# A gated delta-rule block with 2:4-sparse feed-forward: the first step in an order of its own, and part of the feed-forward preparation in the first drain body

## The reference, cut to what matters

```python
mod = silu(c) @ wmod                      # 6 parts of 256: sa, ca, ga, sb, cb, gb, per batch
ga, gb = guard(ga), guard(gb)             # magnitude at least 0.25, sign kept
h = layernorm(x) * (1 + ca) + sa          # x: 8 batches x 256 tokens x 256
# attention, 16 key heads (128), 2 value heads (128) each
qkv, z = h @ W_qkv.T, h @ W_z.T
beta = sigmoid(h @ W_b.T); decay = exp(-softplus(h @ W_a.T + dt_bias) * exp(A_log))
qkv = causal 4-tap convolution of qkv; q, k = l2norm per head
for t in range(256):                      # delta rule, state 128 x 128 for each value head
    dv = beta[t] * (v[t] - k[t] @ S); S = S * decay[t] + outer(k[t], dv); o[t] = q[t] @ S
x = x + ga * ((rmsnorm(o) * norm_w * silu(z)) @ W_out.T)
h = layernorm(x) * (1 + cb) + sb
h = silu(h @ w_gate) * (h @ w_up)         # 1024 wide
h = of every 4 neighbours keep the 2 of largest magnitude
x = x + gb * (h @ w_down)
```

## Time and profile before

| what | value |
|---|---|
| median of 3 runs | 2014.25 us (2011.45 to 2016.29) |
| the profiled execution | 2010.74 us, its span 2009.0 us |
| busy share PE, DVE, ACT, POOL | 97%, 90%, 86%, 69% |
| instructions | 63635 |
| mean granted clock of PE | 0.988 |
| share of PE in the chain that ended last | 91% |

### The profile page before, as it was taken

The page is one execution under the profiler, slowest core; times in us unless marked ns, Lnnn a source line. Parts: engine busy times, 40 slices in busy tenths (PEclk is TensorE's granted clock), DMA queues, the critical chain, the costliest instruction groups (busy, mean ns, idle before and its releaser), DMA issues.

```text
span 2009.0 us, 63635 instructions
## 1 busy us (share of the span) xinstructions
PE 1947.9 (97%) x24518; PEld 1656.9 (82%) x24518; DVE 1800.0 (90%) x2901; ACT 1737.5 (86%) x3588; POOL 1382.2 (69%) x962
## 2 busy tenths in 40 slices
PE   6699999999999999999999999999999999997999
PEld 5478888888888888888888888888888888886787
DVE  6889999999999999999999999999999999985997
ACT  4699999999999999999999999999999999986332
POOL 6367777777777777777777777777777777764452
PEclk9799999999999999999999999999999999998899
DMA  3000000000000000000000000000000000003000
GB/s 117 13 23 3 3 24 3 24 2 24 3 24 3 24 2 4 22 3 23 3 24 3 24 3 24 3 24 2 3 24 3 24 3 2 24 3 115 6 27 22
DMA packets 17596, 35.75 MB, mean 18 GB/s; under 512 B 5772, under 2 KB 14092, under 8 KB 14996
## 3 DMA queue, kind: packets, MB, share of 16 engines
q1 hardware_dynamic: 17300, 31.68, 4.7%
HBM read 29.04 MB, written 2.64 MB: 16 GB/s over the span
## 4 chain that ended last, share of the span: by engine, by line
PE 91%; DVE 3%; POOL 2%; issue 2%; ACT 1%; DMA 0%; POOLq 0%; SPq 0%; DVEq 0%; ACTq 0%
PE bank L647 81%; PE bank L650 10%; DVE tt L1677 0%; ACT yl L1282 0%; DVE b_le L1667 0%; POOL a_lo L520 0%; DMA o<-in_x 0%; POOL go L541 0%; POOL invT L557 0%; POOL y_acc L564 0%; POOL osq L513 0%; DVE ae L1831 0%; DVE oss L1899 0%; POOL f_small L572 0%; POOL e_b L505 0%
## 5 line engine op out<-in xcount | busy, mean ns | idle before, releaser
L1796 DVE SCALAR_TENSOR_TENSOR cc<-bank,wc,cc 128x510 f32<-128x510 f32 (+2 forms) x768 | 558.7, 740 | 13.4 <-ACT cc L1307 3.7
L647 PE MATMUL bank<-h,w 128*128 128x512 f16 (+1 forms) x1920 | 422.4, 361 | 5.6 <-DVE cc L1796 5.5
L647 PEld LDWEIGHTS bank<-h,w 128*128 128x128 f16 x1920 | 173.9, 98 | 140.9 <-DVE cc L1796 6.6
L486 POOL TENSOR_TENSOR rn<-n2m,mhalf 128x4 f32<-128x4 f32 x64 | 64.8, 1012 | 280.8 <-DVE n2m L1812 280.8
L1392 ACT ACTIVATE inv<-bank 128x512 f16<-128x512 f32 x384 | 244.7, 637 | 11.5 <-PE bank L647 11.5
L1397 ACT ACTIVATE invT<-bank 128x512 f16<-128x512 f32 x384 | 246.5, 642 | 1.3 <-PE bank L647 1.3
L1860 DVE TENSOR_TENSOR yl<-bank,mask 128x512 f16<-128x512 f32 x320 | 218.9, 684 | 6.5 <-PE bank L647 6.4
L647 PE MATMUL bank<-inv,a 128*128 128x64 f16 (+1 forms) x3584 | 217.4, 197 | 4.1 <-ACT inv L1392 3.9
L1307 ACT ACTIVATE cc<-bank,wc 128x512 f32<-128x512 f32 x256 | 177.8, 695 | 33.3 <-PE bank L647 33.2
L647 PEld LDWEIGHTS bank<-inv,a 128*128 128x128 f16 x3584 | 179.7, 98 | 16.5 <-ACT inv L1392 5.2
L647 PE MATMUL bank<-w,goT 128*128 128x256 f16 x1536 | 190.8, 275 | 1.4 <-DVE goT L1912 1.4
(11 more groups left out here) (230 smaller groups left out, 5504.1 us busy)
## 6 DMA issues: line engine op xcount, KB each, us to landing
w_raw<-in_wh SPq DMA_DIRECT2D x15, 1032.0 KB, 5.0
v<-in_x SPq DMA_DIRECT2D x4, 512.0 KB, 4.0
out<-sol SPq DMA_DIRECT2D x16, 128.0 KB, 1.7
moving<-rank_store SPq DMA_DIRECT2D x64, 8.0 KB
standing<-rank_store SPq DMA_DIRECT2D x64, 8.0 KB
w_raw<-in_wgate SPq DMA_DIRECT2D x1, 1024.0 KB, 5.0
cc<-in_wup SPq DMA_DIRECT2D x1, 1024.0 KB, 4.8
pt<-gate_store SPq DMA_DIRECT2D x2, 512.0 KB, 5.1
```

Source lines behind the costliest of these rows:

```text
L486: gp.tensor_tensor(rn[:], n2m[:, blk(s), 0], mhalf[:, 0:TL], ALU.pow).then_inc(sig("rn"), 1)
L647: return mm(o_, l_, r_, start=start, stop=stop, skip_group_check=True)
L1796: V.scalar_tensor_tensor(dst, src, wc[:, par(s), i, 3 - j:4 - j], dst, ALU.mult, ALU.add).then_inc(sig(f"conv{i}"), 1)
```

## The change

**Setup.** The constants of `moving` and `standing` are no longer made by four memsets of POOL but by three Copies of ACT from `ones` (signal `rank_rows`): one ahead of the wait for the first input, two ahead of the wait for the first weights. POOL's selects follow `e_b`'s memset at once. ACT's eight `yl` copies move from the first body to the end of ACT's setup; DVE's `level_masks` and `decay_logs` move to the end of DVE's setup, in this order.

**First body.** Each engine has a `first_body` of its own. The reciprocal and the column operations are split: the columns of block 0 in the first body, those of the other three blocks in body 1, on DVE after convolve(1, 3). `guard_gates` moves to body 1, behind `keys_low`. `modulation_rest` moves on PE ahead of `rank_sums`, to banks 2 and 3. SP stores the ranks of block 0, loads step 0's, then stores the rest; the gates' store comes after load_rank(2). POOL's key norm waits for the keys' guarded norm alone, in all steps.

**Drain.** In body 64, `gated(0..3)` stand on DVE behind `level_rows(1)`, `add_input(0..3)` on POOL behind `first_inverse(63)`, the gate weights' low parts a little earlier, and the statistics, normed tiles, transposes (banks 2 and 3) and half of ACT's `hidden_turned` between the other work. `gate(0)`, `up(0)`, `gate_silu(0)` and `hidden_product(0)` move up in body 65. Block 0's gates go to a place of their own (`gates_0` in kn) and block 0's input to e_b, so that their DMAs start earlier; x is loaded in the order 0, 1, 2, then 3 once eight tiles are added. The diff, cut to its core:

```diff
@@ sync
-            sp.dma_start(rank_store, rank_parts).then_inc(sig("gate_dma"), 16)
+            sp.dma_start(rank_store[:, 0], rank_parts[:, 0]).then_inc(sig("gate_dma"), 16)
...
             load_rank(0)
+            sp.dma_start(rank_store[:, 1:NB], rank_parts[:, 1:NB]).then_inc(sig("gate_dma"), 16)
+            sp.wait_ge(sig("gate_dma"), 32)
             load_rank(1)
...
+            sp.wait_ge(sig("knt_ps"), STEPS)
+            sp.dma_start(gates_0, gate_store[0:BG, 0:C].unsqueeze(0).broadcast_to([P, BG, C])).then_inc(sig("f_g0"), 16)
+            sp.wait_ge(sig("at"), STEPS)
+            sp.wait_ge(sig("pt"), STEPS)
+            load_inputs(0)
@@ gpsimd
-            gp.memset(moving[0:HP], LOG_NONE).then_inc(cst, 1)
-            gp.memset(standing[0:HP], 1.0).then_inc(cst, 1)
-            pool.wait_ge(cst, CONSTS - 8)
-            gp.memset(moving[HP:HP + 2 * RANK], -1.0).then_inc(cst, 1)
-            gp.memset(standing[HP:HP + 2 * RANK], 1.0).then_inc(cst, 1)
-            pool.wait_ge(cst, CONSTS - 6)
+            pool.wait_ge(sig("rank_rows"), 3)
...
+            def first_body(s0):
+                queries_low(s0)
+                key_norm(s0)
+                masked_beta(s0)
+                decay_beta(s0)
+                split_weights(s0)
...
                     unit_system(s1)
                     first_inverse(s1)
+                    if not s0:
+                        for j in range(TL):
+                            add_input(j)
...
+                if s1 and not s0:
                     for j in range(TL):
                         hidden_rstd(j)
                     hidden_low(0)
                     hidden_low(1)
+
+            def last_bodies(s0, s1, s2, s3):
+                gate_output(s3)
+                if s2:
+                    scaled_low(s2)
+                output_scale(s3)
+                scaled_output(s3)
+                if s2:
+                    hidden_low(2)
+                    hidden_low(3)
@@ tensor
+            def first_body(s0):
+                project(0, s0)
+                project(1, s0)
+                modulation_rest()
+                rank_sums()
+                bank_project(2, s0, None)
+                project(2, s0)
+                turn_keys(s0)
+                turn_queries(s0)
+                decay_sums()
+                bank_project(3, s0, None)
+                project(3, s0)
+                bank_decays(0, s0, None)
+                decay_product(0, s0)
+                pe.wait_ge(sig("logs_read"), 3)
+                turn_normed(s0)
+                bank_decays(1, s0, None)
+                decay_product(1, s0)
+                key_query(s0)
+                key_key(s0)
...
                     z_rows(0, s1)
+                    if not s0:
+                        turn_hidden(0)
+                        turn_hidden(1)
...
                     first_values(s2)
+                    gate(0)
                     key_state(s2)
...
                     second_values(s2)
-                    turn_hidden(2)
-                    turn_hidden(3)
+                    up(0)
@@ scalar
+            act.wait_ge(sig("pool_const"), 1)
+            every = lambda lo, hi: ones[lo:hi].unsqueeze(1).broadcast_to([hi - lo, 2 * U, P])
+            A(moving[0:HP].rearrange("p r u s -> p (r u) s"), every(0, HP), ACT.Copy, scale=LOG_NONE).then_inc(sig("rank_rows"), 1)
             act.wait_ge(sig("x_dma_0"), 32)
             A(c_th, cT_sb, ACT.Tanh, scale=0.5).then_inc(sig("silu_c"), 1)
...
+            def first_body(s0):
+                last_tap(0, s0)
+                last_tap(1, s0)
+                gates_kept()
+                rank_high()
+                last_tap(2, s0)
+                queries_high(s0)
+                squares(0, s0)
+                squares(1, s0)
+                decay_factors()
+                keys_normed(s0)
+                last_tap(3, s0)
+                decay_exp(0, s0)
+                keys_turned(s0)
+                split_weights(s0)
+                decay_exp(1, s0)
+                inverse_odds(s0)
+                high_half(s0)
...
                     z_tanh(0, s1)
+                    if not s0:
+                        hidden_turned(0)
+                        hidden_turned(1)
@@ vector
+            def first_body(s0):
+                for j in range(1, TAPS):
+                    convolve(0, j, s0)
+                rank_low()
+                for j in range(1, TAPS):
+                    convolve(1, j, s0)
+                modulation(1, bank[3][:, 0:32])
+                for j in range(1, TAPS):
+                    convolve(2, j, s0)
+                squared_norms(0, s0)
+                guarded_keys(s0)
+                beta_columns(0, early)
+                step_columns(0, early)
+                for j in range(1, TAPS):
+                    convolve(3, j, s0)
+                keys_low(s0)
+                squared_norms(1, s0)
+                guarded_queries(s0)
+                level_masks_diagonal()
+                dve.wait_ge(sig("mask_done"), 2)
+                decayed_queries(s0)
+                decayed_keys(s0)
...
                     convolve(1, 3, s0)
+                    if N(s0) == 1:
+                        beta_columns(1, late)
+                        step_columns(1, late)
                 if s1:
                     level_rows(1, s1)
+                    if not s0:
+                        for j in range(TL):
+                            gated(j)
+                        gate_weights_low(0)
+                        gate_weights_low(1)
...
             def last_bodies(s0, s1, s2, s3):
                 if s2:
-                    for j in range(TL):
-                        hidden_stats(j)
-                    for j in range(TL):
-                        hidden_normed(j)
                     up_weights_low(0)
                     up_weights_low(1)
+                    second_rest(s2)
```

More of the change, by code:

```diff
@@ L40 @@
 RANK = 4
-CONSTS = 22
+CONSTS = 18
 W_SCALE = 64.0
@@ L1267, in _ @@
             A(dtb_b, bank[7][:, 256:256 + NV], ACT.Copy).then_inc(sig("rows_ready"), 1)
+            act.wait_ge(sig("same_ps"), 1)
+            for u in range(U):
+                A(yl[:, :, u], ident16[:].unsqueeze(1).broadcast_to([P, NL, P]), ACT.Copy).then_inc(sig("yl_ready"), 1)
             act.wait_ge(sig("ba_done"), 5)
@@ L1785, in _ @@
             decay_columns()
+            level_masks()
+            decay_logs()
             def convolve(i, j, s):
```

232 lines of the change are left out of this document (112 added, 120 removed).

## The result

The changed kernel takes **2016.38 us** (median of 22 runs, 2012.64 to 2018.73) against 2011.30 us for the kernel before beside it (22 runs): ratio 1.0022, 95% interval [1.0015, 1.0028]. The profiled execution took 2014.39 us, its span 2012.7 (before: 2010.74 and 2009.0).

The account below looks back on a forecast made before the run. Steady bodies are PE-bound and the closing feed-forward loop DVE-bound, both unchanged. Start -6.5 us and drain +5 sum to -1.5 us; on the median of 2014.25 us, forecast 2012.5 us, range 2004 to 2020.

Parts of the forecast that it names:

- Setup: Setup: without POOL's memsets, DVE's last normed tile ends at 25.0 us, -2.7 us (bounds 0 and -5.5).
- decay_logs: First step: with level_masks ahead and the convolutions behind, decay_logs ends at 47.4 instead of 53.2 us, -5.8 in all.
- Clock ahead of the rank sums: First step: PE's clock holds through a 2.2 us wait; if not, rank sums and project(2) cost 3.6 us more.
- First decayed_keys: Setup and first step together: the first decayed_keys ends 12.5 us earlier (-10 to -14).
- Body 1: Body 1 pays back +6.0 us: late columns +3.8, guard_gates +1.9, PE's clock 0.3.
- Start in all: Setup, first step and body 1 together: -6.5 us (-3 to -9).
- POOL's wait: Body 64: POOL waits for gated tiles before adding, scaled_low comes late and PE's key_state(62) waits, +7.8 us.
- hidden_turned: Body 64: the hidden_turned(0..1) pair stands before inverse_left(4) on ACT, +2.3 us.
- Bodies 65, 66: Bodies 65, 66: second_values(63) sooner -4.5, up(0) and gate_silu(0) ahead of u1(63) +1.6, hidden_low and hidden_product(0) moved -2.2 us.
- Drain in all: Bodies 64 to 66 together: +5.3 us (+1 to +9), taken as 5.
- Slower: Drain rival, chance 0.24: POOL's wait, then PE at half clock in body 64, gate(0), up(0); drain +9 or +10, 2019 us.
- The constants bring nothing: Setup rival, chance 0.05: selects hold DVE as the memsets did; start -3.8 us, time 2015 us.

Follow-up runs that it names:

- e1: Kernel before with only the start's half of the change (setup, first step, body 1, gate store), drain as before; 2005.98 us, ratio 0.9964.
- e3: Changed kernel with POOL's add_input(0..3) of body 64 moved behind output_scale, low_half, scaled_low and scaled_output; 2012.09 us, ratio 1.0004.
- e4: Kernel before with only the rank constants moved from POOL's memsets to ScalarE's Copies; 2007.07 us, ratio 0.9974.
- e12: Changed kernel with POOL's additions late, scaled_output before scaled_low, DVE's gatings behind second_rest, late columns split over bodies 1 and 2; 2007.97 us, ratio 0.9986.
- e16: As e15, but with the columns split as in the changed kernel; 2002.46 us, ratio 0.9955.
- the four filled ones: e11, e14, e15 and e16: PE's setup wait for the last normed tile filled with eight repeated gate products; the 48 products took 5.5 to 5.8 us.
- e14: As e4, with PE's setup wait for the last normed tile filled by 8 repeated gate-product matmuls; 2005.55 us, ratio 0.9971.
- e11: As e1, with late columns split over bodies 1 and 2 and PE's setup wait filled by 8 repeated gate-product matmuls; 2006.41 us, ratio 0.9979.
- e15: Changed kernel with columns whole in the first step, PE's setup wait filled, and the drain's work placed as in e12; 1997.15 us, ratio 0.9933.

## Why the prediction was wrong, by its steps

The mechanisms that it names were there, but the sum had the sign wrong by the size of three terms. In body 1 it took PE's clock at 0.3 us where the rows show about 4. In bodies 65 and 66 it took -5.1 us where they gave -2.4, above all because PE waits there for `go`. And it took half clock behind the pause of body 64 at a net 0.4 us: the body became 11.2 us longer, 0.8 more than forecast. The profile of after hides the first of the three behind a luck of 4.3 us. The 0.8 us of the middle, which it took as unchanged, no run explains.

- **Setup** (-2.7 us, bounds 0 and -5.5): -4.0, with DVE beside the selects at 4.39 us for the four tiles instead of 8.67. The mechanism was right and the size off. In the other profiles with ScalarE's constants the four tiles took 5.3 us, a gain of 3.3. The sentence on the port lock, that the gain would be nearer to 2 us than to 5, fits those, and not the 4.0 of after.
- **The gate products**: I counted them at 10.15 us on both sides. The profile of after had 4.3 us of luck that no step of mine foresaw; in e1, with the same setup, they took 10.34. This may be why the profiles stand 3.7 us apart and the medians 5.1; the other executions of after were not profiled.
- **decay_logs** at 47.4: 43.3 in after, 48.3 in e1. The `yl` copies did lie in ACT's idle time: they end at 36.1, when the input of Exp is ready too. Without the luck the step was right to 0.9 us. **Clock ahead of the rank sums**: I assumed no fall; it fell (0.50), and the rank sums took 3.74 us where I had counted 2.3 (in before they took 3.78). The wait was 5.61 us in after; but in e1 it was 1.93, less than the 2.2 that I counted, and the clock fell there too (0.73 in 48 to 50), so the argument from a shorter wait failed, and not the wait alone.
- **First decayed_keys** (-12.5): -15.4 in after, with the luck, -11.9 in e1. Right.
- **Body 1** (+6.0): +9.5 in after, +8.9 in e1. The late columns took 4.45 us against 3.8. guard_gates took 2.4, but its net cost is 1.3 against 1.9, since `decayed_queries` waited 1.04 us for e_b in before. The step that failed is "PE's clock: ... 0 to 1.7; I take 0.3". PE waits 3.80 us at the start of the body (0.36 in before), project(1) then takes 2.75 us instead of 1.46, and DVE reaches the columns 1.2 us later than in before. Behind the columns PE pauses 3.35 us and works at half clock from 81 to 95 us, and the way to `keys_low` takes 14.3 us instead of 11.4. The worse error was to take the split as a given: whole columns cost the first step 2.0 us, not the 3.2 that their length adds, since DVE otherwise waits there twice (0.76 and 0.78 us in e1).
- **Start in all** (-6.5): -5.9 in after with the products' luck, -3.0 in e1's profile; by its runs e1 gives 5 (medians) to 7 (ratio, 4 to 10), with a part of it from the drain's scatter.
- **POOL's wait** (+7.8) in body 64: PE's wait of 8.91 us in place of 0.35. Right. **hidden_turned** (+2.3): the pair took 2.4 us on ACT. With half clock behind the pause body 64 became 11.2 us longer (10.4). e3 shows what I missed: DVE's gatings take twice as long beside POOL's products (5.09 us), and that work does not "lie in PE's time" once the first wait is gone.
- **Bodies 65, 66** (-4.5 + 1.6 - 2.2 = -5.1): -2.4. `second_values(63)` gained 2.8 instead of 4.5, because PE now stands 2.97 us for `go`, behind `scaled_low(63)` on POOL, a queue order that I did not cost; up(0) then ran at half clock and cost 2.45 instead of 1.6. **Drain in all** (+5.3, taken as 5): +8.8.
- **The rivals**: "Slower", at 0.24, came true in its sign, its place and the price of the drain (+8.8 for 9 or 10), but only in part by its mechanism. Its price rests on half clock through body 64, gate(0) and up(0); the clock of after is back at 1.00 from 1815, reads 1.00 under gate(0) at 1835 and 0.50 under up(0) until 1849, behind the wait for `go`. PE's groups between 1811 and 1815 are 1.7 us longer than in before, and in bodies 65 and 66 before had its half clock too, so most of the 8.8 us is the wait of 8.91 itself. Of its 2019 us the runs show 2016.4. In 1805 to 1811 the clock of after reads 0.50 with PE idle:
```profile
1805.00:1811.00 6.00, 0.00 (x0) 0.50 0.15 61
1811.00:1817.00 6.00, 5.25 (x50) 0.67 0.12 14
```
By the warning against pauses in the Trainium skill (TensorE: Matmul & The Clock Gate; it stands in "Why this matters for your kernels", not in the section that the prediction named), this rival should have had the larger chance: the change makes long pauses of PE in two places, and the traces agree in both. My error was to price half clock at 0.3 us in body 1 and 0.4 in the drain and to keep the rest for the rival, although showed it in the same stretch. "The constants bring nothing", at 0.05, fell: e4 gives 5 us (3 to 7).

## What to carry to other kernels

Before splitting an operation so as to shorten a chain, look whether its engine waits on that chain: here it saved 2.0 us on the chain, and the part moved into a gapless run cost 6.4. When work is put into an in-order queue, price the first thing behind it that the bound engine needs, then that engine's half clock after the pause, and look for the next wait before counting the gain of removing one. Try the parts of a many-part change alone: the one simple edit (constants to the engine that idles) carried a gain that the rest hid. And profile the same code more than once before explaining a difference of 4 us: the gate products and the gatings of the drain both came out in two ways here.

## What the runs showed of the hardware

- The granted clock reads 1.00 in the whole setup, and yet 128x64 f32 matmuls take 10.34 us for 48 in one execution and 5.90 in another of the same setup. The Trainium skill (TensorE: Matmul & The Clock Gate, "What's actually happening") says that the number of slow matmuls at a kernel's start varies from run to run; the traces agree.
- DVE's four gatings (two SBUF inputs) took 5.09 us in all in e3 beside POOL's products and 1.42 in e12, where POOL's four additions took 5.97 us instead of the 3.71 of e16: one engine's gain is the other's loss. The Trainium skill (SBUF — State Buffer, "SBUF: two separate sides") has a lock on the port pair that the two share, held for a whole instruction; these rows agree:
```profile
1810.04 1.42 DVE L2022 SCALAR_TENSOR_TENSOR y_acc<-y_acc,kn 128x256 f32<-128x256 f32 x4
```
- Even a 4-column TENSOR_SCALAR, 0.17 us elsewhere, took 2.32 us at 60.70 in after, beside POOL's e_b of 2.35 us.
- In the setup PE's products were fast in the five profiles in which it hardly waited ahead of the last turn before them (0.1 us in after, and the four filled ones) and slow in 14 of the 15 in which it waited there for 0.7 to 4.4 us. Why e3 was fast behind 0.89 us, and why e14 and e16 turned fast one group of matmuls later than e11 and e15, stays open.
